# Three in place of four GpSimd products in the third layer of slot b, the fourth as a single item on VectorE

## The reference

```python
xk = x0                                   # (1024, 32, 16)
outs = []
for W in (W0, W1, W2):                    # (32, 32|64, 64)
    xk = relu(einsum('bmd,bhd,mhk->bkd', x0, xk, W))
    outs.append(sum(xk, axis=2))
z = concatenate(outs, axis=1)             # (1024, 192)
h = concatenate([z, dense_ctx], axis=1)   # (1024, 208)
h = maximum(h @ W_top1 + b_top1, 0)
h = maximum(h @ W_top2 + b_top2, 0)
y = h @ W_top3
```

## Time and profile before

| what | value |
|---|---|
| median of three runs | 620.44 us (620.21 to 620.96) |
| the profiled execution, whole | 619.78 us |
| its span, first to last instruction | 618.0 us |
| PE busy | 562.0 us (91%) |
| DVE busy | 554.5 us (90%) |
| POOL busy | 468.6 us (76%) |
| ACT busy | 299.5 us (48%) |
| granted TensorE clock, mean | 0.994 of full speed |

### The profile page before, as it was taken

One profiled execution on the slowest core, in us unless ns is written; L12 is line 12 of the kernel. 1 busy time (PEld: TensorE's weight loads), 2 busy tenths in 40 slices (PEclk: granted clock), 3 DMA queues, 4 the chain that ended last, 5 costly groups with the idle time before them and its releaser, 6 DMA issues.

```text
span 618.0 us, 8180 instructions
## 1 busy us (share of the span) xinstructions
PE 562.0 (91%) x2752; PEld 206.1 (33%) x2752; DVE 554.5 (90%) x281; ACT 299.5 (48%) x1366; POOL 468.6 (76%) x354
## 2 busy tenths in 40 slices
PE   0058889999999999999999999899998999999997
PEld 0012222334333443334333433234332433334334
DVE  0067899999999999999999999989998999999991
ACT  0021607574357535674366535674346544774331
POOL 6748888888888888888888888888888885125450
PEclk9998999999999999999999999999999999999999
DMA  6297979792699819893699719793498809892000
GB/s 171 79 382 254 394 250 396 241 397 82 209 359 330 294 51 374 297 399 108 218 351 339 299 40 379 265 400 130 171 397 309 329 3 319 316 406 100 1 2 0
DMA packets 54252, 152.02 MB, mean 246 GB/s; under 512 B 9697, under 2 KB 18913, under 8 KB 54210
## 3 DMA queue, kind: packets, MB, share of 16 engines
q1 hardware_dynamic: 46018, 149.39, 64.7%
q0 software_dynamic: 8192, 2.11, 2.6%
HBM read 147.26 MB, written 4.20 MB: 245 GB/s over the span
## 4 chain that ended last, share of the span: by engine, by line
PE 48%; POOL 23%; DVE 10%; issue 9%; DMA 6%; SPq 1%; ACT 1%; DVEq 0%; POOLq 0%
PE acc L570 43%; POOL emb L323 14%; DVE zd L406 10%; POOL zg L335 9%; DMA rolled<-x_scratch 5%; PE mlp L613 2%; SPq L287 1%; PE mlp L604 1%; PE mlp L605 1%; PE acc L579 1%; PE mlp L620 0%; DVE zpart L382 0%; PE mlp L586 0%; ACT xk_sb L472 0%; DMA emb<-tables_in,index 0%
## 5 line engine op out<-in xcount | busy, mean ns | idle before, releaser
L406 DVE TENSOR_TENSOR zd<-rolled,xk_ps 128x2048 f32<-128x2048 f32 x239 | 530.0, 2279 | 16.2 <-PE acc L570 9.2
L570 PE MATMUL acc<-zd,w_sb 128*64 128x512 f32 x1672 | 384.6, 597 | 8.4 <-DVE zd L406 8.4
L323 POOL DMA_INDIRECT emb<-tables_in,index x256 | 244.6, 955 | 75.3 <-issue 64.3
L335 POOL TENSOR_TENSOR zg<-rolled,xk_sb 128x1024 f32<-128x1024 f32 x94 | 223.8, 2382 | 52.0 <-ACT xk_sb L472 18.9
L570 PEld LDWEIGHTS acc<-zd,w_sb 128*64 128x64 f32 x1672 | 119.7, 138 | 242.5 <-issue 210.4
L472 ACT ACTIVATE xk_sb<-acc 64x512 f32<-64x512 f32 x128 | 75.7, 591 | 64.4 <-PE acc L570 61.9
L570 PE MATMUL acc<-zg,w_sb 128*64 128x512 f32 x376 | 98.6, 601 | 6.9 <-POOL zg L335 6.9
L570 PE MATMUL acc<-zd,w 128*64 128x512 f32 x256 | 61.6, 601 | 37.4 <-DVE zd L406 37.4
L472 ACT ACTIVATE xk_ps<-acc 64x512 f32<-64x512 f32 x126 | 71.8, 570 | 30.1 <-PE acc L570 27.2
L451 ACT ACTIVATE relu_ab<-acc 128x16 f32<-128x16 f32 x480 | 78.9, 294 | 8.3 <-PE acc L570 8.3
L451 ACT ACTIVATION_READ_ACCUMULATOR relu_ab<-acc 128x1 f32 x480 | 79.3, 322 | 0.0
(11 more groups left out here) (45 smaller groups left out, 101.0 us busy)
## 6 DMA issues: line engine op xcount, KB each, us to landing
rolled<-x_scratch SPq DMA_DIRECT2D x256, 512.0 KB, 9.4
base<-x_scratch SPq DMA_DIRECT2D x16, 512.0 KB
emb<-tables_in,index POOLq DMA_INDIRECT x256
x_scratch<-emb SPq DMA_DIRECT2D x32, 128.0 KB
w_sb<-w_in SPq DMA_DIRECT2D x2, 512.0 KB, 4.9
wt<-wtop_in SPq DMA_DIRECT2D x1, 512.0 KB, 6.3
wt1a<-wtop_in SPq DMA_DIRECT2D x1, 256.0 KB, 5.5
w<-w0a_in SPq DMA_DIRECT2D x1, 160.0 KB, 2.3
```

Of the source, the lines that this page charges most:

```text
L323: pool.indirect_dma_start(emb[:, i % 2, c * DIM:(c + 1) * DIM], None, tables, bass.IndirectOffsetOnAxis(index[:, g:g + 1].bitcast(U32), 0) ...
L335: nc.gpsimd.tensor_tensor(zg[:, n % ZG_BUFS, :], rolled[:, s, j, :], xk_sb[:, s, :], ALU.mult).then_inc(zg_ready, 1)
L406: nc.vector.tensor_tensor(zd[:, n % ZD_BUFS, 0:w, :], rolled[:, s, j:j + w, :], repeated(layer_in, w), ALU.mult).then_inc(zd_ready, 1)
L570: end = nc.tensor.matmul(acc[h * MAPS:(h + 1) * MAPS, bank, :], weights, z[:, h * HALF:(h + 1) * HALF], start=(j + c == 0), stop=(i == len ...
```

## The change

In the second part of slot b's third layer (phase (b',2,1) in every tile), DVE takes chunks 5 to 13 and POOL chunks 14 and 15. Before, DVE took 5 to 12 and POOL 13 to 15. Nine chunks are four items of two and one item of one, since `Plan` steps by two. With the chunk of the phase's first part, POOL has three in place of four. The seven gathers that follow POOL's products in this phase are dealt out as 3 and 4, in place of 2, 2 and 3. The last odd stream (15) has its own entry in `CHUNKS_AT` and keeps its split, so that seven phases change, of streams 1, 3, ..., 13.

```diff
 CHUNKS = {(0, 0): [(4, 0)], (0, 1): [(4, 0), (10, 2)], (0, 2): [(12, 4)],
-          (1, 0): [(4, 0)], (1, 1): [(14, 2)], (1, 2): [(4, 1), (8, 3)]}
+          (1, 0): [(4, 0)], (1, 1): [(14, 2)], (1, 2): [(4, 1), (9, 2)]}
...
-GATHERS_AFTER = {(0, 1, 1): [3, 3], (1, 1, 0): [3, 3], (0, 2, 0): [3, 3, 2, 2], (1, 2, 0): [3], (1, 2, 1): [2, 2, 3]}
+GATHERS_AFTER = {(0, 1, 1): [3, 3], (1, 1, 0): [3, 3], (0, 2, 0): [3, 3, 2, 2], (1, 2, 0): [3], (1, 2, 1): [3, 4]}
```

## The result

The changed kernel takes 624.4 us (median of 11 runs, 622.06 to 627.94) against 620.96 us (median of 11, 619.77 to 622.40) for the kernel before. The ratio is 1.0057, with a 95% interval of 1.004 to 1.0075. The forecast was 624.2 us. The measured rise is 3.4 us, with an interval of 2.5 to 4.7, and the forecast one was 3.8.

The account below looks back on a forecast made before the run. DVE and PE in turns bound the short tiles, POOL's 71.2 us period the long ones. First tile +1.13 and six tiles +2.68 made +3.81 on 619.78, 623.6 us, so 624.2 us for the median, range 622.6 to 626.4.

Parts of the forecast that it names:

- The loop of DVE and PE: In the short middle tiles DVE and PE are late in turns; the period goes from 69.36 to 70.49 us.
- The price of the single item: DVE's added 128x1024 product in phase (b',2,1) costs 1.13 us per tile, 7.9 us for seven phases.
- POOL's relief: One product less per tile saves POOL 2.26 us, its period falling from 71.21 to 68.95 us, so long tiles shorten.
- The 4.10 us that go: The 0.33, 1.85, 1.83 and 0.09 us by which four middle tiles exceed 69.36 us vanish with POOL's shorter period.
- The first tile: From 81 to 154.8 us, bounded by DVE alone; it grows by 1.13 us.
- What moved and cost nothing: Moved sum of (a,0), PE's order, ACT's copy and chunk reloads around the phase's end: no cost on the path.
- A: DVE's 0.87 us of waits per tile take the item in: tiles 69.62 us, total 619.0 us; chance 0.07.
- B: The item is hidden altogether and POOL's relief stays: all tiles 69.36 us, -4.1 us, 616.3 us; chance 0.04.
- C: Transfers of `rolled` set the long tiles, so every tile adds 1.13: +7.9 us, 628.4 us; chance 0.09.

Follow-up runs that it names:

- e1: Kernel before plus an unread DVE sum over 1024 columns in phase (b',2,1) of seven tiles, POOL's work kept: 624.62 us, ratio 1.0079.
- e3: Changed kernel with the three additional gathers per tile in the first two tiles only, as in e2: 623.98 us, ratio 1.0062.
- e4: e1 with the three additional gathers per tile in the first two tiles only, as in e2: 623.42 us, ratio 1.005.
- e5: Changed kernel with its single item made as wide as a pair (chunk 13 twice, one used): 631.12 us, ratio 1.0176 to before.
- e2: Kernel before with the three additional gathers per tile in the first two tiles instead of five, nine others moved later: 618.38 us, ratio 0.9975.
- before_again: Kernel before, unchanged, run once more for a second trace: 620.04 us against 620.02 in 23 other runs.
- e8: e2 plus an unread DVE sum over 1024 columns, taking no zd buffer, in phase (b,1,0) of seven tiles: 619.68 us, ratio 0.9993.

## Why the prediction was right, and where it was not

**The loop of DVE and PE.** Right. The period was given as 70.49 us, and four tiles of the changed kernel, all six of e1 and all but one each of e3 and e4 (70.59 and 70.54) measure that. e5 shows the slope. That the median came within 0.2 us of the forecast is in part luck: the 3.8 us were added to a median of three runs, 620.44, where eleven have 620.96, and the two profiled executions differ by 5.5 us.

**The price of the single item.** Right: 1.13 us from start to start by the line through rows of 2048 and 512 columns, 1.13 measured. Its own duration, 1.220 us, is longer, but 0.09 us of it overlap with the instruction behind. So the duration is no price here. It is near the 1.225 of the single items from SBUF, and near the 1.224 that the formula of the Trainium skill ("VectorE: DVE Perf Modes", section on the TRN2 errata) gives as an estimate.

**POOL's relief.** The size was about right, the reason wrong. The prediction's step that a product less for POOL shortens the long tiles, and that "without that cover POOL's bound would be 71.2 again", fell with e1: with all of POOL's work in place the tiles are 70.49 too. The long tiles went because a slower loop no longer overtakes POOL. What POOL gave up bought nothing in these six tiles: they take 422.92 us in e1, with all of POOL's work, and 423.66 in the changed kernel. The prediction also dated POOL's bound too late, "from about 385 us on". In the trace of before PE waits for POOL one tile earlier, and the 0.33 us of the third tile are that:

```profile
329.89 1.08 PE L570 MATMUL acc<-zg,w_sb 128*64 128x512 f32 x4 [0.55 <-POOL zg L335]
```

**The 4.10 us that go.** That POOL's rate set them in the trace of before was right (e2, before_again). As a term of a sum over tiles they were taken from one trace in which nothing else was late. In the second trace of before, POOL's clock also hid waits of 0.44 and 1.14 us for transfers, so how much the relief is worth depends on the run. Of the 3.40 us that the six tiles grew, 2.68 were forecast. The other 0.72 are two DVE waits, one of 0.21 for `rolled` at 482.04 and one of 0.59 at 277.22, which the trace puts on a PE that had released that buffer 2.6 us before. What DVE waited for there stays open.

**The first tile.** +1.13 was forecast and the two traces show +2.11. The traces of the kernels with the same DVE work in it (the change, e1, e3, e4) have 156.11 to 157.76, and those with before's DVE work in it have 154.80 and 152.79 (before) and 156.20 (e2). The excess is of the size by which runs of one kernel differ there, and the single item's share can't be separated from it.

**What moved and cost nothing.** Right as far as seen: the sum behind the single item starts at once (192.18, DVE without a gap), and DVE's waits at the tile's start are still 0.39 and 0.48. The forecast that all six tiles are alike within 0.2 us was too narrow. PE's waits were to grow by about 1.1 us in a tile and grew by 0.56, from 0.22 to 0.78. The rest shows as busy time, 69.71 us in place of 69.14 for the same 346 matmuls, whose ends are modelled. Why it is split so stays open.

**The rivals.** A (waits take the item in) and B fell by the tiles. So did C as a cause of the two long tiles of the earlier trace rows, by e1 and e2 too, though a tile of the second trace of before is long (71.12 us) in part by transfers. e8 shows that A's mechanism works in the phase (b,1,0), at 69.43 us and not 69.62.

The Trainium skill, "GPSIMD Engine Reference", section Engine selection, puts elementwise multiplies on VectorE and calls GpSimd about twice as slow. The traces confirm the ratio, 2.38 us to 1.13 per chunk. The kernel still got slower, since GpSimd's time was free in these tiles and VectorE's was not.

## What to carry to other kernels

Two engines that feed each other through a few buffers can both be over 98% busy, as here, and each be the bound for a part of the loop. Added work cost its whole length in the part where its engine is late (1.13 us of 1.13) and nearly nothing in the other (0.1), so find, for the place of an edit, which wait comes next behind it. An engine whose own rate becomes the bound only after it has lost a lead isn't worth relieving by an edit that slows the others. And count buffers by item: moving a half-filled one into a phase cost up to 0.77 us per loop more than the same time without a buffer.

## What the runs showed that I had not expected

The kernel before has a third limit close behind the other two, the transfers. With POOL out of the way (e2) the loads of slot b came 0.4 us late twice in one tile, in a second trace of the unchanged kernel 0.44 and 1.14 us. In the changed kernel's loop of 70.49 us the trace shows only 0.21 us of them. So moving nine gathers gained 1.5 us (0.9975 of before) and not the 4.1 that POOL's waits promised, and e2 still has the lowest ratio of all kernels here.
